# Two value tables with the far embedding in them, a plain transpose of the output, and chunks 10 slots apart

## The chip, the cores and the metric

The program runs on one core of a Trainium2 chip. The metric is the device time of one execution, in microseconds. Five engines take part: TensorE (PE, with its weight loads shown apart as PEld), VectorE (DVE), ScalarE (ACT), GpSimd (POOL) and the DMA queue of SyncE (SP). Each engine runs its own list of instructions in order and waits on semaphores for the others.

## The reference

```python
# x: (8, 1024, 256), 16 heads of 16 columns, relative distances clipped to -64..64
def attn(x):                                   # x is layernorm(x)
    q, k, v = (x @ W.T + b, split into heads)
    logits = q @ k.T + einsum('bhqd,qkd->bhqk', q, embK[clip(k - q) + 64])
    w = softmax(logits)
    out = w @ v + einsum('bhqk,qkd->bhqd', w, embV[clip(k - q) + 64])
    return out @ Wo.T + bo
x = x + layernorm(attn(layernorm(x)))
x = x + layernorm(layernorm(x) @ (ternary(Wf) * alpha).T + bf)
```

For a key more than 64 tokens away, the row of embV that is added is always the first (far to the left) or the last (far to the right). These two rows are "the far embedding". Since every weight of a query is used once, the far part of the output is: the sum of the weights on the left side times embV[0], plus the sum on the right side times embV[128].

## The kernel before, in words

A batch has 1024 tokens, in 8 tiles of 128 and in 4 chunks of 256. The 16 heads are two groups of 8. A step `s` is one query tile of one group of one batch, so there are 8 x 2 x 8 = 128 steps; 4 steps are a quad, 2 a pair. Per head of a step, TensorE computes a row of scores for the maximum (`row_max`, L736), DVE adds the band and takes the maximum of the two halves (L1013, L1016), TensorE computes the logits again transposed (`weights`, L759 and L764), ACT takes the exponent (L1216), and TensorE multiplies the weights with the values (`weighted`, L797). Four heads lie side by side in 32 rows each of the PSUM bank `oacc`.

The values lie in a ring of `VRING` = 4 buffers `vs`, one for each group of a batch. A head has 16 columns of value and 2 columns of ones. A tile on the left of the query takes 17 of these columns (`VL`), one on the right takes all 18 (`VR`), so that row 16 of the result is the sum of all weights and row 17 the sum of those on the right. Because row 17 is written by tiles on the right alone, the product starts with such a tile (`turns`), and for query tile 0 a matmul with zeros (L782) comes first. `out_copy` (ACT, L1223) moves a pair to `oT`, `relative` and `relative_sum` add the near embedding, and `out_norm` (L834) turns `oT` with a matmul against the 128x128 table `outmap`: the identity, with rows 16 and 17 of each head block holding the far embedding. DVE then divides by the sum (L1064, L1072).

The next batch is prepared in chunks beside the attention of the present one. The stages of a chunk are `load_x` (SP), `statistics` (DVE, then the root on POOL, L1244 to L1254), `normalise` (POOL, L869), `turn_x` (L683), `project_q` and `project_k` (L693), `far` (L701), `project_v` (L710), whose result DVE moves with the bias added to `vs` (L994, two instructions), the split into three bf16 parts on POOL (L885 to L893), and the writes to DRAM by SP (`write_q`, `write_far`, `write_k`; L502, L566), from which `load_q` and `load_k` fetch what the attention needs. `fraw`, a scratch of `far`, is a part of the chunk's input buffer `xc`. After the second group of a batch, each of its tiles goes through a tail: `tail_wo`, `tail_x1`, `tail_norm`, `tail_normed`, `tail_x1T`, `tail_ff`, `tail_out`, with three more roots on POOL.

The order of work on each engine is planned before the kernel is built. `timetable` (L105) gives each stage a slot; a batch of attention is 128 slots; `with_banks` moves a stage to a later slot when none of the three PSUM banks `misc` is free (with held times such as 1.8 slots for `project_v`), `LAG` adds an engine's delay, and each engine's list is the stages sorted by slot. A slot is no time: it only sets the order. The chunks of the next batch start at slots 40, 53, 72 and 85 of the present one. The tails of a batch take slots 101 to 173 from its start, so the last ones fall in slots 0 to 45 of the next batch. `relative` of a quad stands at its slot 29.6 on, `relative_sum` at 33, `out_norm` at 34.8 and 36.

Of the kernel before, what the change touches and what calls it, by code (L numbers as in the profile page):

```python
# [18 lines left out]
G = 2  # L19
# [16 lines left out]
VL, VR = D + 1, D + 2  # L36
# [5 lines left out]
QRING, BRING, VRING = 5, 7, 4  # L42
# [62 lines left out]
def timetable():  # L105
# [204 lines left out]
def build(nc, a, out):  # L310
    with ExitStack() as ctx:
# [17 lines left out]
        bv = sb("bv", [P, H])  # L329
        outmap = sb("outmap", [P, P])  # L330
# [3 lines left out]
        headmask, kfar = sb("headmask", [P, 32]), sb("kfar", [P, 2])  # L334
# [8 lines left out]
        vs = [sb(f"vs{i}", [P, T, HG, VR]) for i in range(VRING)]  # L343
# [25 lines left out]
        fraw = xc[:, 0, 0:P]  # L369
# [29 lines left out]
        band_cleared, ones_set, outmap_ready = sem("band_cleared"), sem("ones_set"), sem("outmap_ready")  # L399
# [16 lines left out]
        N_CONST, N_TABLE, N_ZERO = 8, 12, 8  # L416
# [90 lines left out]
        def sync_program(e):  # L507
# [5 lines left out]
            for t_, name in ((bq, "bq"), (bk, "bk"), (headmask, "headmask"), (kfar, "kfar")):  # L513
                e.dma_start(t_[:], a[name]).then_inc(const_in, 16)
            e.dma_start(bv[:], a["bv"].partition_broadcast(P)).then_inc(const_in, 16)
# [4 lines left out]
            for t_, name in ((later[:], "later"), (outmap[:], "outbase"), (zbuf[0][:, 0:P], "outleft")):  # L520
                e.dma_start(t_, a[name]).then_inc(table_in, 16)
            for t_, name in ((relmask[:], "relmask"), (relsel[:], "relsel"), (partmask, "partmask"), (embk6, "embk6")):
                e.dma_start(t_, a[name]).then_inc(table_in, 16)
# [16 lines left out]
            for stage, k in order:  # L540
# [120 lines left out]
        def tensor_program(e):  # L661
            pe, order = Engine(e), orders["PE"]
            for stage, k in order:
# [103 lines left out]
                elif stage == "weighted":  # L767
# [8 lines left out]
                    zero = zeros[:].bitcast(BF16)  # L776
# [586 lines left out]
```

## Time and profile before

| | us |
|---|---|
| three runs, median | 2812.86 |
| lowest, highest | 2808.33, 2814.58 |
| the profiled execution | 2808.32 |
| its span | 2806.5 |

The span is the time from the first to the last instruction in the trace, 1.8 us less than the execution's own time. The profile's page has one line for each view; the numbers behind an instruction are its busy time (in which instructions of one group that overlap count once), the mean length of one, and the idle time of the engine ahead of it. Matmuls overlap, so the length of one (some 275 ns) says little on how often one can start. What one costs is read from the distance of starts in the timeline.

### The profile page before, as it was taken

Reading aid. Unit: us, or ns where it says so; the run is one execution under the profiler, and the core shown is the slowest. Engines: PE = TensorE matmul, PEld = TensorE weight load, DVE = VectorE, ACT = ScalarE, POOL = GpSimd, SP = SyncE. Lnnn points to the kernel's source line nnn. Section 1 sums busy time; section 2 is a strip of 40 time slices with the busy share of each in tenths; the row PEclk is TensorE's granted clock in tenths of the full one; section 3 lists DMA queues with packets and bytes.
Section 4 is the critical chain, followed back from the end, with each engine's and each line's share of the span. In section 5 each row is a group of like instructions: output and inputs, shape, how many; then the busy total and the mean of one; then the engine's idle time right before and its main releaser. Section 6 shows DMA issues by size and latency. Waiting matters only on the chain.

```text
span 2806.5 us, 102954 instructions
## 1 busy us (share of the span) xinstructions
PE 2611.6 (93%) x43410; PEld 1965.8 (70%) x43410; DVE 2034.6 (72%) x5187; ACT 1557.5 (55%) x2993; POOL 959.2 (34%) x2275
## 2 busy tenths in 40 slices
PE   5899999999999999999999999999999999999995
PEld 3577777677776777767776777767777677777773
DVE  3776678776786778866787667876678766787774
ACT  2455556455555555555555565545665455565651
POOL 3113333433334323343234332334323433341026
PEclk8799999999999999999999999999999999999997
DMA  7556654456455564455645556446554456545410
GB/s 221 174 137 178 170 150 131 129 154 187 124 151 138 160 166 134 135 157 156 175 116 145 156 157 169 117 131 177 163 144 131 121 171 181 145 132 144 134 44 28
DMA packets 605048, 409.11 MB, mean 146 GB/s; under 512 B 149162, under 2 KB 604330, under 8 KB 604330
## 3 DMA queue, kind: packets, MB, share of 16 engines
q1 hardware_dynamic: 604586, 402.54, 50.7%
q8 instruction: 341, 5.59, 0.9%
q14 instruction: 121, 0.99, 0.1%
HBM read 206.84 MB, written 194.90 MB: 143 GB/s over the span
## 4 chain that ended last, share of the span: by engine, by line
PE 69%; DVE 16%; issue 5%; ACT 4%; POOL 3%; SPq 2%; DMA 1%; DVEq 0%; ACTq 0%; POOLq 0%
PE oacc L797 15%; PE logitsT L759 15%; PE scores L736 14%; PE logitsT L764 7%; DVE maxes L1016 6%; DVE junk L1013 5%; PE misc L860 4%; PE misc L693 4%; PE misc L822 2%; PE misc L834 2%; PE misc L710 2%; PE misc L810 2%; ACT wxr L1216 2%; POOL rs L1249 1%; PE misc L720 1%
## 5 line engine op out<-in xcount | busy, mean ns | idle before, releaser
L1013 DVE CUSTOM_DVE_ANT_1 junk<-scores,bands 128x512 bf16<-128x512 f32 x988 | 679.6, 688 | 585.3 <-PE scores L736 566.7
L759 PE MATMUL logitsT<-qs,ks 98*128 98x128 bf16 (+3 forms) x9088 | 994.9, 215 | 32.4 <-ACT wxr L1216 23.3
L1216 ACT ACTIVATE wxr<-logitsT 128x512 f32<-128x512 f32 x1024 | 599.8, 601 | 559.4 <-PE logitsT L759 463.0
L759 PEld LDWEIGHTS logitsT<-qs,ks 98*128 98x128 bf16 (+1 forms) x9088 | 679.5, 99 | 253.2 <-issue 92.8
L1216 ACT ACTIVATE wy<-logitsT 128x512 f32<-128x512 f32 x1024 | 587.4, 597 | 431.7 <-PE logitsT L759 421.3
L736 PE MATMUL scores<-ks,qs 101*128 101x256 bf16 (+10 forms) x4096 | 719.2, 291 | 77.3 <-DVE maxes L1016 38.4
L1016 DVE TENSOR_REDUCE maxes<-scores 128x1 f32<-128x512 f32 x1024 | 701.6, 685 | 1.9 <-PE scores L736 1.9
L736 PEld LDWEIGHTS scores<-ks,qs 96*128 96x128 bf16 (+3 forms) x4096 | 299.1, 99 | 263.7 <-DVE maxes L1016 119.5
L764 PE MATMUL logitsT<-ident,bands 128*128 128x128 f32 x2048 | 467.6, 280 | 0.0
L1244 POOL TENSOR_SCALAR rs<-rs 128x1 int32<-128x1 int32 (+1 forms) x224 | 48.6, 217 | 981.3 <-DVE rs L924 978.7
L764 PEld LDWEIGHTS logitsT<-ident,bands 128*128 128x128 f32 x2048 | 292.3, 143 | 33.2 <-issue 0.4
L1249 POOL TENSOR_SCALAR rs<-rs 128x1 f32<-128x1 f32 x768 | 292.4, 384 | 67.0
L797 PE MATMUL oacc<-wy,vs 128*17 128x128 f32 (+3 forms) x9216 | 276.5, 263 | 0.9 <-ACT wy L1216 0.9
L797 PE MATMUL oacc<-wxr,vs 128*18 128x128 f32 (+3 forms) x9216 | 276.6, 263 | 0.2
L797 PEld LDWEIGHTS oacc<-wy,vs 128*17 128x17 f32 (+1 forms) x9216 | 207.0, 98 | 45.2 <-issue 19.8
L1254 POOL TENSOR_SCALAR rs<-rs 128x1 f32<-128x1 f32 x768 | 212.0, 279 | 68.4
L797 PEld LDWEIGHTS oacc<-wxr,vs 128*18 128x18 f32 (+1 forms) x9216 | 206.9, 98 | 38.5 <-issue 23.5
L1038 DVE COPY_PREDICATED wxr<-later,wxr 128x512 f32<-128x512 int32 x224 | 174.8, 781 | 6.5 <-PE oacc L797 6.1
L1193 ACT ACTIVATE praw<-misc 128x512 f32<-128x512 f32 x256 | 152.7, 597 | 30.0 <-DMA bs<-praw 15.5
L1194 ACT ACTIVATE praw<-misc 128x512 f32<-128x512 f32 x256 | 155.4, 607 | 0.0
L1304 POOL TENSOR_TENSOR x<-ybuf,x 128x256 f32<-128x256 f32 x60 | 47.0, 783 | 192.5 <-DVE ybuf L1095 188.1
L810 PE MATMUL misc<-wxr,reltab 128*32 128x64 f32 x4096 | 102.9, 241 | 6.0 <-DVE wxr L1041 2.1
(136 smaller groups left out, 2561.5 us busy)
## 6 DMA issues: line engine op xcount, KB each, us to landing
bs<-praw SPq DMA_DIRECT2D x256, 512.0 KB, 4.3
bands<-bs SPq DMA_DIRECT2D x224, 512.0 KB, 4.3
ks<-kd SPq DMA_DIRECT2D x64, 384.0 KB, 5.0
qs<-qd SPq DMA_DIRECT2D x112, 192.0 KB
bands<-bs SPq DMA_DIRECT2D x128, 128.0 KB, 3.7
qd<-qparts SPq DMA_DIRECT2D x64, 192.0 KB, 3.2
kd<-kparts SPq DMA_DIRECT2D x64, 192.0 KB, 2.6
qd<-qparts SPq DMA_DIRECT2D x64, 128.0 KB, 2.6
```

The source lines that it names most:

```text
L736: mm = e.matmul(scores[r0:r1, c:c + length], qs[i][0:depth, h, r0:r1], kk[0:depth, h, key:key + length], start=True, stop=True, skip_group ...
L759: mm = e.matmul(lt[:, c * P + q0:c * P + q1], kk[0:depth, h, kt * P:(kt + 1) * P], qs[i][0:depth, h, q0:q1], start=q0 == 0, stop=not near, ...
L764: mm = e.matmul(lt[:, c * P:(c + 1) * P], band[v % BRING][:, h % HB, c * P:(c + 1) * P], ident[:], start=False, stop=True, is_transpose=Tr ...
L797: mm = e.matmul(oacc[32 * j:32 * j + (VR if right else VL), o0 + q0:o0 + q1], vs[m_ % VRING][:, kt, h, 0:VR if right else VL], src, start= ...
L810: mm = e.matmul(m[32 * j:32 * j + 32, o0:o0 + QUAD * HG * 2], reltab[:, 126 - q:128 - q, :].rearrange("p n d -> p (n d)"), wx[:, :, :, P + ...
L1013: e.tensor_tensor_reduce(junk[:], scores[:, 0:512].rearrange("p (a c) -> p a c", a=2), banded, 1.0, LOWEST, ALU.add, ALU.max, mx[:, h, 0:1 ...
L1016: e.tensor_reduce(mx[:, h, 1:2], scores[:, 512:S], AX.X, ALU.max).then_inc(row_maxed, 1)
L1038: e.copy_predicated(right, mask.bitcast(I32), left).then_inc(merged, 1)
L1194: e.activation(dst[:, :, P:WIN], src[:, :, P - 1:P].broadcast_to([P, HB, P]), ACT.Copy).then_inc(praw_ready, 1)
L1216: e.activation(dst, src, ACT.Exp).then_inc(exp_ready, 1)
L1249: op = e.tensor_scalar(rs[k][:, 3, x:x + 1], rs[k][:, 2, x:x + 1], rs[k][:, 0, x:x + 1], rs[k][:, 2, x:x + 1], ALU.mult, ALU.mult)
L1254: op = e.tensor_scalar(rs[k][:, 2, x:x + 1], rs[k][:, 3, x:x + 1], 1.5, rs[k][:, 2, x:x + 1], ALU.add, ALU.mult)
```

## The change

The values get two versions for each group, one for tiles on the left with bias + embV[0], one for tiles on the right with bias + embV[128]. Each has 16 columns of value and 1 of ones (`VW` = 17). All products have 17 rows, the matmul with zeros and the order `turns` go, and `out_norm` is a transpose by the identity. DVE writes four instructions for a chunk in place of two. The ring has 3 buffers. The chunks start at slots 61, 71, 81 and 91, with `project_k` and `write_k` 2 slots sooner within a chunk. `fraw` has a buffer of its own, and `load_x` no longer waits for `far`. At the start one more constant is loaded (`farV`, two rows broadcast to 128 partitions) and two tables less.

```diff
-VL, VR = D + 1, D + 2
+VW = D + 1
-QRING, BRING, VRING = 5, 7, 4
+QRING, BRING, VRING = 5, 7, 3
...
-            first = (b - 1) * G * T * HG + (40, 53, 72, 85)[c] if b else 10 * c - 100
+            first = (b - 1) * G * T * HG + (61, 71, 81, 91)[c] if b else 10 * c - 100
...
-                                 (2.3, "project_v"), (3.9, "far"), (6.5, "write_q"), (10.3, "project_k"),
-                                 (7, "write_far"), (13, "write_k")):
+                                 (2.3, "project_v"), (3.9, "far"), (6.5, "write_q"), (8.3, "project_k"),
+                                 (7, "write_far"), (11, "write_k")):
...
-        bv = sb("bv", [P, H])
-        outmap = sb("outmap", [P, P])
+        bvs = sb("bvs", [P, 2, H])
...
-        vs = [sb(f"vs{i}", [P, T, HG, VR]) for i in range(VRING)]
+        vs = [sb(f"vs{i}", [P, 2, T, HG, VW]) for i in range(VRING)]
...
-        fraw = xc[:, 0, 0:P]
+        fraw = sb("fraw", [P, P])[:]
+        headmask = fraw[:, 0:32]
...
-        N_CONST, N_TABLE, N_ZERO = 8, 12, 8
+        N_CONST, N_TABLE, N_ZERO = 9, 10, 8
...
-            e.dma_start(bv[:], a["bv"].partition_broadcast(P)).then_inc(const_in, 16)
+            e.dma_start(zbuf[0][:], a["bv"].partition_broadcast(P)).then_inc(const_in, 16)
+            e.dma_start(bvs[:].rearrange("p a h -> p (a h)"), a["farV"].partition_broadcast(P)).then_inc(const_in, 16)
...
-            for t_, name in ((later[:], "later"), (outmap[:], "outbase"), (zbuf[0][:, 0:P], "outleft")):
...
                     sp.wait_ge(x_turned, n("x_turned", "turn_x", b, c) - 1)
-                    sp.wait_ge(far_ready, b * NCHUNK + c)
                     e.dma_start(xc[:], xrow[b, c]).then_inc(x_in, 16)
...
-                    if kind == "X" and blk == 0 and t == 0:
-                        pe.wait_ge(band_cleared, 1)
-                        cols = oacc[:].rearrange("p (i q) -> p i q", i=4)[:, s % 2 * 2:s % 2 * 2 + 2, 0:HALF]
-                        e.matmul(cols, zero[:, 0:P], zero[:, 0:P], start=first, stop=True, skip_group_check=True)
-                        first = False
...
-                    turns = [1, 2, 3, 0] if kind == "X" and t else range(4)
-                    for x, c in enumerate(turns):
-                        kt = tiles[c]
+                    for c, kt in enumerate(tiles):
...
-                                mm = e.matmul(oacc[32 * j:32 * j + (VR if right else VL), o0 + q0:o0 + q1],
-                                              vs[m_ % VRING][:, kt, h, 0:VR if right else VL], src, start=first and x == 0,
-                                              stop=True, skip_group_check=True)
+                                mm = e.matmul(oacc[32 * j:32 * j + VW, o0 + q0:o0 + q1], vs[m_ % VRING][:, int(right), kt, h, :],
+                                              src, start=first and c == 0, stop=True, skip_group_check=True)
...
-                            mm = e.matmul(m[:, o0:o0 + P], oT[:, blk, pair % 2 * 2 + i, :], outmap[:], start=True, stop=True)
+                            mm = e.matmul(m[:, o0:o0 + P], oT[:, blk, pair % 2 * 2 + i, :], ident[:], start=True, stop=True,
+                                          is_transpose=True)
...
+                    e.tensor_tensor(bvs[:], bvs[:], zbuf[0][:].rearrange("p (a h) -> p a h", a=1).broadcast_to([P, 2, H]),
+                                    ALU.add).then_inc(bvs_ready, 1)
...
-                    then_step(e.tensor_tensor(outmap[:], outmap[:], zbuf[0][:, 0:P], ALU.subtract))
-                    dve.wait_ge(dve_step, step[0])
-                    e.tensor_tensor(outmap[:], outmap[:], ident[:], ALU.add).then_inc(outmap_ready, 1)
...
-                        op = e.tensor_tensor(
-                            vs[m_ % VRING][:, c * CHUNK:(c + 1) * CHUNK, :, 0:D],
-                            m[:, 0:CHUNK * H].rearrange("p (i g h d) -> p g i h d", i=CHUNK, g=G, h=HG)[:, g],
-                            bv[:, g * P:(g + 1) * P].rearrange("p (a h d) -> p a h d", a=1, h=HG)
-                            .broadcast_to([P, CHUNK, HG, D]), ALU.add)
+                        for side in range(2):
+                            op = e.tensor_tensor(
+                                vs[m_ % VRING][:, side, c * CHUNK:(c + 1) * CHUNK, :, 0:D],
+                                m[:, 0:CHUNK * H].rearrange("p (i g h d) -> p g i h d", i=CHUNK, g=G, h=HG)[:, g],
+                                bvs[:, side, g * P:(g + 1) * P].rearrange("p (a h d) -> p a h d", a=1, h=HG)
+                                .broadcast_to([P, CHUNK, HG, D]), ALU.add)
...
+        "farV": np.concatenate([np.tile(embV[0], NH), np.tile(embV[-1], NH)]),
```

## Rows read from the trace of the kernel before

**Rows 1.** The profile's page: busy time by engine, chain by engine.
```profile
PE 2611.6 (93%) x43410; PEld 1965.8 (70%) x43410; DVE 2034.6 (72%) x5187; ACT 1557.5 (55%) x2993; POOL 959.2 (34%) x2275
...
PE 69%; DVE 16%; issue 5%; ACT 4%; POOL 3%; SPq 2%; DMA 1%; DVEq 0%; ACTq 0%; POOLq 0%
```

**Rows 2.** Window of one batch: stretch, busy us of each engine, granted clock, DMA.
```profile
776.00:1114.00 338.00, 321.88 (x5428) 243.34 (x5426) 250.73 (x641) 192.75 (x372) 123.84 (x289) 1.00 0.53 149
```

**Rows 3.** Waits of the whole span, those of PE on DVE.
```profile
PE scores L736 <- DVE maxes L1016: 38.4, 185, 0.4
PE scores L736 <- DVE maxes L1013: 27.6, 58, 1.6
```

**Rows 4.** Timeline of PE: product with outmap, a transpose of four, what follows each.
```profile
1021.66 1.05 PE L834 MATMUL misc<-outmap,oT 128*128 128x128 f32 x8
1022.55 0.39 PE L759 MATMUL logitsT<-qs,ks 98*128 98x128 bf16 x4
...
902.46 0.61 PE L683 MATMUL misc<-ident,xc 128*128 128x128 f32 x4
902.90 0.39 PE L720 MATMUL misc<-bandtab,qs 96*128 96x128 bf16 x4
```

**Rows 5.** Groups by line: the output's product and the transposes.
```profile
L764 PE MATMUL logitsT<-ident,bands 128*128 128x128 f32 x2048 | 467.6, 280 | 0.0
...
L834 PE MATMUL misc<-outmap,oT 128*128 128x128 f32 x512 | 70.3, 280 | 7.9 <-DVE zbuf L1124 5.8 <-DVE oT L1056 2.1
```

**Rows 6.** Timeline of PE around the matmul with zeros.
```profile
236.75 0.22 PE L782 MATMUL oacc<-bands 128*128 128x128 bf16 x1
236.90 0.81 PE L797 MATMUL oacc<-wxr,vs 128*17 128x64 f32 x44
```

**Rows 7.** Groups by line: the value products of 18 and of 17 columns.
```profile
L797 PE MATMUL oacc<-wxr,vs 128*18 128x128 f32 x4608 | 170.8, 276 | 0.0
...
L797 PE MATMUL oacc<-wy,vs 128*17 128x128 f32 x4608 | 164.0, 276 | 0.0
```

**Rows 8.** DVE moves a chunk's values: timeline of one chunk.
```profile
878.74 0.75 DVE L994 TENSOR_TENSOR vs<-misc,bv 128x256 f32<-128x256 f32 x2
```

**Rows 9.** Windows of 26 us: two phases, each with chunks, then without.
```profile
848.00:874.00 26.00, 22.64 (x296) 16.28 (x291) 18.54 (x52) 13.06 (x25) 12.68 (x31) 1.00 0.33 91
2538.00:2564.00 26.00, 25.07 (x382) 18.60 (x381) 21.47 (x58) 15.81 (x29) 6.65 (x18) 1.00 0.40 112
...
900.00:926.00 26.00, 25.38 (x581) 20.03 (x581) 18.56 (x44) 16.26 (x33) 8.09 (x11) 1.00 0.57 172
2590.00:2616.00 26.00, 25.30 (x679) 19.57 (x678) 21.45 (x53) 13.23 (x25) 0.00 (x0) 1.00 0.46 135
```

**Rows 10.** Timeline near 860 us: two roots on POOL, then DVE and PE.
```profile
853.16 0.19 POOL L1244 TENSOR_SCALAR rs<-rs 128x2 int32<-128x2 int32 x1 [0.43 <-DVE rs L924]
856.15 0.15 DVE L924 TENSOR_SCALAR rs<-mv 128x1 f32<-128x1 f32 x1
858.03 0.19 POOL L1244 TENSOR_SCALAR rs<-rs 128x1 int32<-128x1 int32 x1
860.77 0.79 DVE L1117 TENSOR_SCALAR zbuf<-x,mv,rs 128x256 f32<-128x256 f32 x1 [1.03 <-POOL rs L1254]
862.23 0.39 PE L736 MATMUL scores<-ks,qs 96*128 96x256 bf16 x2 [1.59 <-DVE maxes L1013]
```

**Rows 11.** Timeline of one chunk after its transpose at 902.46 us: ACT, SP, POOL.
```profile
909.14 0.83 ACT L1171 ACTIVATE qf<-misc,bq 128x256 f32<-128x256 f32 x2
926.81 1.36 SPq L566 DMA_DIRECT2D qd<-kparts  x4
930.44 0.85 ACT L1171 ACTIVATE qf<-misc,bk 128x256 f32<-128x256 f32 x2 [5.53 <-PE misc L693]
933.99 1.16 POOL L893 TENSOR_TENSOR kparts<-qf,kparts 128x512 bf16<-128x512 f32 x1
```

**Rows 12.** Chain of waits at the start of the span.
```profile
12.61 4.74 DMA alpha<-in_alpha
```

More of the change, by code:

```diff
@@ L333, in build @@
         relmask, relsel = sb("relmask", [P, 2]), sb("relsel", [P, 4, 32])
-        headmask, kfar = sb("headmask", [P, 32]), sb("kfar", [P, 2])
+        kfar = sb("kfar", [P, 2])
         farw = sb("farw", [P, 32])
@@ L398, in build @@
         far_first, far_second, far_ready = sem("far_first"), sem("far_second"), sem("far_ready")
-        band_cleared, ones_set, outmap_ready = sem("band_cleared"), sem("ones_set"), sem("outmap_ready")
+        band_cleared, ones_set, bvs_ready = sem("band_cleared"), sem("ones_set"), sem("bvs_ready")
         farw_ready, k_ones_in, v_ones_set, junk_set = sem("farw_ready"), sem("k_ones_in"), sem("v_ones_set"), sem("junk_set")
@@ L512, in sync_program @@
                 e.dma_start(t_[:], a[name].rearrange("(i p) o -> p i o", p=P)).then_inc(const_in, 16)
-            for t_, name in ((bq, "bq"), (bk, "bk"), (headmask, "headmask"), (kfar, "kfar")):
-                e.dma_start(t_[:], a[name]).then_inc(const_in, 16)
-            e.dma_start(bv[:], a["bv"].partition_broadcast(P)).then_inc(const_in, 16)
+            for t_, name in ((bq[:], "bq"), (bk[:], "bk"), (headmask, "headmask"), (kfar[:], "kfar")):
+                e.dma_start(t_, a[name]).then_inc(const_in, 16)
+            e.dma_start(zbuf[0][:], a["bv"].partition_broadcast(P)).then_inc(const_in, 16)
+            e.dma_start(bvs[:].rearrange("p a h -> p (a h)"), a["farV"].partition_broadcast(P)).then_inc(const_in, 16)
             for c in range(1, NCHUNK):
@@ L519, in sync_program @@
                 e.dma_start(t_[:], a[name].rearrange("(i p) o -> p i o", p=P)).then_inc(table_in, 16)
-            for t_, name in ((later[:], "later"), (outmap[:], "outbase"), (zbuf[0][:, 0:P], "outleft")):
-                e.dma_start(t_, a[name]).then_inc(table_in, 16)
-            for t_, name in ((relmask[:], "relmask"), (relsel[:], "relsel"), (partmask, "partmask"), (embk6, "embk6")):
+            for t_, name in ((later[:], "later"), (relmask[:], "relmask"), (relsel[:], "relsel"), (partmask, "partmask"), (embk6, "embk6")):
                 e.dma_start(t_, a[name]).then_inc(table_in, 16)
@@ L775, in tensor_program @@
                     pe.wait_ge(v_ones_set, 1)
-                    zero = zeros[:].bitcast(BF16)
                     if first and s >= 2:
                         pe.wait_ge(o_copied, s // 2)
-                    if kind == "X" and blk == 0 and t == 0:
-                        pe.wait_ge(band_cleared, 1)
-                        cols = oacc[:].rearrange("p (i q) -> p i q", i=4)[:, s % 2 * 2:s % 2 * 2 + 2, 0:HALF]
-                        e.matmul(cols, zero[:, 0:P], zero[:, 0:P], start=first, stop=True, skip_group_check=True)
-                        first = False
                     o0 = (s % 2 * 2 + blk) * P
-                    turns = [1, 2, 3, 0] if kind == "X" and t else range(4)
-                    for x, c in enumerate(turns):
-                        kt = tiles[c]
+                    for c, kt in enumerate(tiles):
                         for q0, q1, right in value_sides(t, kt):
@@ L828, in tensor_program @@
                     pe.wait_ge(o_added, 2 * (pair // 2) + 2)
-                    pe.wait_ge(outmap_ready, 1)
                     pe.wait_ge(*free)
@@ L933, in vector_program @@
                     dve.wait_ge(dve_step, step[0])
-                    e.tensor_scalar(farw[:], headmask[:], small[:, 4:5], None, ALU.mult).then_inc(farw_ready, 1)
+                    e.tensor_scalar(farw[:], headmask, small[:, 4:5], None, ALU.mult).then_inc(farw_ready, 1)
+                    e.tensor_tensor(bvs[:], bvs[:], zbuf[0][:].rearrange("p (a h) -> p a h", a=1).broadcast_to([P, 2, H]),
+                                    ALU.add).then_inc(bvs_ready, 1)
                 elif stage == "tables":
@@ L989, in vector_program @@
                     dve.wait_ge(v_summed, n("v_summed", "project_v", b, c))
+                    dve.wait_ge(bvs_ready, 1)
                     for g in range(G):
@@ L1264, in pool_program @@
             for t_ in vs:
-                op = e.memset(t_[:, :, :, D:VR], 1.0)
+                op = e.memset(t_[:, :, :, :, D:VW].rearrange("p a t h c -> p (a t h) c"), 1.0)
             op.then_inc(v_ones_set, 1)
@@ L1333 @@
     f32 = np.float32
-    outbase, outleft = np.zeros((P, P), f32), np.zeros((P, P), f32)
-    for r in range(0, P, 32):
-        outbase[r + D, r:r + D], outbase[r + D + 1, r:r + D], outleft[r + D + 1, r:r + D] = embV[0], embV[-1], embV[0]
     ins = {
```

3 lines of the change are left out of this document (removed).

## The prediction

> **What bounds the kernel now.** I read the page first: PE is busy 93% of the span, DVE 72%, and the chain that ended last lies to 69% on PE and to 16% on DVE [rows 1]. The windows say that this is even: in the 338 us of one batch PE is busy 321.9 us at a granted clock of 1.00, DVE 250.7 us, POOL 123.8 us [rows 2]. So a slot is 338 / 128 = 2.64 us, PE idles 16 us in a batch, and what is taken off PE comes off the span unless PE then waits. The waits show for what: for DVE's maxima, 38.4 + 27.6 = 66 us over the whole span, in 243 short pieces [rows 3]. DVE is thus the second bound, near enough that what is added to it can't be free everywhere. The last view is windows of the same phase in different batches, which show where PE idles more than elsewhere [rows 9].
>
> **Part 1, the transpose in out_norm.** The product with `outmap` takes 8 matmul instructions for 4 tiles; from its first start to the next instruction's is 1022.55 - 1021.66 = 0.89 us. Four float32 transposes by the identity, the same shapes, take 902.90 - 902.46 = 0.44 us [rows 4]. The saving is 0.45 us for each pair, and there are 64 pairs: 28.8 us of PE. Some will be lost where PE came to the pair late by a wait on DVE (7.9 us of idle in all ahead of L834 [rows 5]); half of the pairs stand among tails, where DVE is fuller. I take 90%, -26 us; bounds -29 and -18.
>
> On this the Trainium skill speaks twice. Trace first: L764 makes 2048 float32 transposes of 128x128 of 280 ns each, but they keep PE busy for only 467.6 us, 228 ns each with their overlaps [rows 5], in windows whose granted clock is 1.00 [rows 2]. The page "TensorE: Matmul & The Clock Gate", Part 4: PE-mode transpose, says that a transpose takes about 275 ns in a kernel and doesn't count as PE activity for the clock. By the length alone, paid in full, the sum would not fall but rise (a rival below). The table of terms of the same page says that the transpose mode is 4 times faster for float32; by that the pair would fall from 0.89 to 0.22 us, and the sum would be 14 us better than mine. The rows show a factor of two.
>
> **Part 2, the values.** A product of 18 columns costs what one of 17 does, 276 ns both [rows 7]; the columns are not what PE is paid for, so the uniform 17 give nothing. The matmuls with zeros are 16, each 236.90 - 236.75 = 0.15 us to the next start [rows 6]: -2.4 us, I take -2. The order of the four tiles changes no count.
>
> DVE pays. Two instructions for a chunk's values take 0.75 us with their overlap [rows 8]; four take 2 x 0.75 less one overlap, about 1.43 us. That is +0.68 us for each of 32 chunks, 21.8 us of DVE. Behind them in DVE's list stand the next maxima, for which PE waits. Outside the tails DVE is busy 18.56 of 26 us [rows 9], so it has room to catch up within some microseconds; the cover is that idle time. PE's waits for DVE are 66 of 2806 us, and mostly beside tails, from which the new slots stay away. I take a sixth, +3.5 us; bounds 0 and +21.8. The bank that holds the product is freed 0.7 us later, inside the 1.8 slots (4.8 us) that the planner holds it.
>
> The ring of three buffers brings a wait on the products of the group three before. For the second group of the next batch that is the first group of the present one, whose last product has slot 53.6 + 3.5 + 4.1 = 61.2. `project_v` of the first chunk has slot 63.3 on PE, behind it in the same list, and DVE needs that result anyway. The wait is over when it is reached: 0. From slot 40 it would not have been, which is why the chunks move.
>
> **Part 3, the chunks at slots 61 to 91.** This is the part with a gain that the words of the change don't name. At 848 to 874 us (slots 33 to 43 of a batch) a chunk's statistics meet the last tails, and PE is busy 22.64 of 26 us. In the last batch, which has these tails but no next chunk, the same phase (2538 to 2564) shows 25.07 [rows 9]. The mechanism can be read in one place: POOL starts the root of the chunk at 853.16 and that of the tail only at 858.03, though its input was there at 856.15 + 0.15; DVE waits for it 1.03 us at 860.77, and PE 1.59 us for DVE at 862.23 [rows 10]. The new first chunk starts 21 slots later, when no tail is near. That is 2.43 us in each of the six batches that have both: -14.6 us. What chunks cost elsewhere: with a chunk PE is busy 25.38 of 26 us, at the same phase without any 25.30 [rows 9], so PE does them with no idle time of their own. Against the gain stands the other end: the last chunk's work now runs to slot 102, and the first tail begins at 101. The split of its keys on POOL (slot 101.3) is still ahead of the tail's first root (103.8). Two chunks now also fall on `relative` (slots 61.6 and 93.6); by slots this shifts `project_v` by 0.4 at most, and PE has the work of both to do in any order. I take -11 us; bounds -17 and +10.
>
> `load_x` without its wait and `fraw` apart take nothing off the path: with 10 slots between chunks the old wait would also have been over. 0.
>
> **Part 4, the start.** SP issues 10 table loads for 12, and one constant more. What PE waits for is the last one, `alpha`, issued at 12.61 and landed 4.74 us later [rows 12]; it is issued one load earlier, some 0.5 us. The add of `farV` (about 0.7 us of DVE) falls into DVE's wait for the root of the second chunk. -0.5 us; bounds -1 and +1.5.
>
> **The sum.** -26 - 2 + 3.5 - 11 - 0.5 = -36 us. The profiled execution took 2808.3 us (span 2806.5 and 1.8 around it), which gives 2772. It is the lowest of the range of runs; their median is 2812.9, from which the same sum gives 2777. I say 2775, and reckon the rivals from the same 2811.
>
> **The rivals.** (a) The move is worth nothing, since the new place has collisions of its own: -26 - 2 + 3.5 - 0.5 = -25, 2786. For it: POOL's list holds the key split just ahead of the tail's root. Against: in the chunkless batch the PE idles no less than with chunks [rows 9]. (b) DVE becomes the bound and all of its 21.8 us show: -36 + 18 = -18, 2793. For it the 66 us of waits; against, DVE's idle quarter in [rows 2]. (c) Transposes are paid at their length [rows 5]: 256 x 0.28 = 72 us for 64 x 0.89 = 57 now, so +15 for -26, and the sum is +5, 2816. That is the change not doing what it says. Against it the starts 0.44 / 4 = 0.11 us apart in [rows 4]. (d) **the other side:** chunks 10 slots (26.4 us) apart have no slack. ACT may not take the next chunk's queries out of PSUM before POOL has split the keys of this one. Counted from the transpose, ACT did that 6.7 us in, so for the next chunk it is due 26.4 + 6.7 = 33.1 us in. The keys came to POOL 28.8 us in, now 2 slots sooner, 23.5; the split took 3.8 us (to 935.15) and ended 32.7 us in, now at best 27.4. But it overwrites the buffer from which SP sends the far part, and SP had done issuing that at 25.7 us in [rows 11]; with 0 to 4.7 us to land (the latter is the small load of [rows 12]), the split starts at 25.7 to 30.4, say 28, and ends 3.8 us later, at 31.9. The slack is 1.2 us, within 5.7 and -1.1. If SP is later by more than that, ACT stands, exponents stop, and PE, which may run two blocks of logits ahead, stops too. There are 21 such passages (3 in each of 7 batches). From 1.8 us lost in each (36 / 21) the change is no gain; at 3 us it is -36 + 63 = +27, 2838. For it: SP is in order, and the example's SP was late by a wait for the maxima. Against: the attention's own SP work is no more than before, and the example is one with SP late.
>
> **How the numbers follow.** The forecast with its own range (2760 to 2786) has 0.58, (a) 0.16, (b) 0.08, (c) 0.04, (d) 0.07, and 0.07 that both savings come in full or more (-29 - 2.4 - 17 with the start, down to 2755). The range is 2756 to 2803: it takes in (a) and (b), and leaves out (c), (d) and the ends. A change within 0.2% (5.6 us) can't be told from none by such runs. Faster by more has 0.88, within it 0.06, which is (c) and a mild (d), slower 0.06.
>
> **What would show it.** `out_norm` with 256 matmul instructions for 512, and 0.44 us from its start to the next instruction. `vs` written by 128 DVE instructions, DVE busy some 20 us more. No L782. PE busy some 31 us less in all, and the window at slots 33 to 43 at about 25 of 26 us. Waits of PE for `maxes` that grow by less than 4 us. I am wrong in part 3 if a new hole in PE stands at slots 95 to 105 or ACT waits for POOL's split; in part 2 if PE's waits for DVE grow by 10 us or more; in part 1 if transposes start 0.2 us apart.

## The result, and the profile after

The changed kernel takes 2816.66 us (median of 20 runs, 2811.64 to 2822.67), the kernel before in the same sitting 2809.61 us (20 runs, 2805.70 to 2815.82). The ratio is 1.0024, with an interval from 1.0017 to 1.0031: slower by 0.24%, or 7 us. I had forecast 2775 us and a range of 2756 to 2803; both are wrong, and so is the sign. Of the twelve executions of one experiment below, the doubled add at the old slots, one took 4688.02 us, in a slower state, and counts in no ratio.

The page of the changed kernel, its span, busy time by engine and chain by engine, against [rows 1]:

```profile
span 2813.6 us, 102464 instructions
...
PE 2588.7 (92%) x43138; PEld 1933.5 (69%) x43138; DVE 2057.9 (73%) x5250; ACT 1558.8 (55%) x2993; POOL 953.6 (34%) x2274
...
PE 60%; DVE 26%; issue 6%; ACT 4%; POOL 2%; SPq 1%; DMA 1%; DVEq 0%; POOLq 0%; ACTq 0%
```

PE lost 22.9 us of work (2611.6 to 2588.7) and the span still grew by 7.1: PE's idle time went from 194.9 to 224.9 us, +30. DVE gained 23.3 us of work, and its share of the chain rose from 16% to 26%. Something that had cover before has none now. The waits of PE on DVE, which answer to [rows 3]:

```profile
PE scores L734 <- DVE maxes L1004: 46.5, 224, 0.4
PE scores L734 <- DVE maxes L1001: 30.1, 69, 1.5
```

They grew from 66.0 to 76.6 us, so of the 30 us of new idle time 10.6 stand here; the rest is spread over smaller waits. Two of these are for PSUM banks that DVE has yet to empty, in seven places each: ahead of `project_v` (L708), a wait that the kernel before does not have, and ahead of `relative` (L799), which with one version of the values (an experiment below) is the last row:

```profile
PE misc L708 <- DVE relout L1035: 6.5, 7, 0.9
PE misc L799 <- DVE vs L982: 6.4, 7, 0.9
...
PE misc L799 <- DVE vs L982: 1.7, 7, 0.2
```

Groups by line of the changed kernel (busy us, mean ns of one | idle before, releaser), the first of which answers to [rows 5]; of before, the merge of the mask, COPY_PREDICATED on DVE, is the last row below:

```profile
L822 PE MATMUL misc<-ident,oT 128*128 128x128 f32 x256 | 39.8, 278 | 13.7 <-DVE zbuf L1112 5.8 <-ACT praw L1182 4.6 <-DVE oT L1044 3.3
L799 PE MATMUL misc<-wxr,reltab 128*32 128x64 f32 x4096 | 101.7, 241 | 10.4 <-DVE vs L982 6.4 <-DVE wxr L1029 1.9 <-DVE wxr L1026 1.7
L982 DVE TENSOR_TENSOR vs<-misc,bvs 128x256 f32<-128x256 f32 x128 | 45.0, 414 | 0.0
L1026 DVE COPY_PREDICATED wxr<-later,wxr 128x512 f32<-128x512 int32 x224 | 191.1, 853 | 12.6 <-PE oacc L787 12.6
```

```profile
L1038 DVE COPY_PREDICATED wxr<-later,wxr 128x512 f32<-128x512 int32 x224 | 174.8, 781 | 6.5 <-PE oacc L797 6.1
```

`out_norm` has its 256 matmuls, and PE comes late to them: 13.7 us of idle time for 7.9. The 128 adds are there. What I had not looked for is the merge: the same 224 instructions take 16.3 us more than before.

To see where in a batch the time goes, I cut each of batches 1 to 6 at the first `out_norm` instruction of each query quad (about slots 34.8, 66.8, 98.8 and 130.8) and took the mean length and, in brackets, the mean of all idle time of PE in each piece (batches 2 to 6 for the first piece). The pieces are named by their slots; nearly all of the new chunks' work lies in the last three. Each row is of one execution, so differences of some 0.1 us say nothing. In us, with the experiments of the next section beside them:

```
kernel                 to 34.8       35 to 67      67 to 99      99 to 131     batch
before                 82.45 (4.50)  90.66 (4.75)  82.30 (3.03)  83.06 (3.44)  338.47
transpose alone        82.11 (5.06)  91.19 (5.41)  82.08 (3.47)  82.13 (3.47)  337.51
new slots alone        82.77 (4.52)  81.04 (3.73)  88.19 (3.20)  85.56 (4.04)  337.56
slots + second add     82.19 (4.52)  81.70 (4.17)  91.55 (5.34)  85.74 (4.14)  341.18
after, one version     82.10 (5.06)  81.36 (4.61)  87.10 (3.21)  84.59 (4.03)  335.16
after                  82.41 (5.06)  81.68 (4.79)  90.57 (5.37)  84.73 (4.08)  339.39
```

### The profile page after: what moved, and what is told of

The parts are those of the page before. It is cut to its first block, busy times and chain, and to the rows that moved or that the text cites. A ratio compares the mean times of both kernels' runs of the same rounds, so it can differ in the third digit from the quotient of the medians.

```text
span 2813.6 us, 102464 instructions
## 1 busy us (share of the span) xinstructions
PE 2588.7 (92%) x43138; PEld 1933.5 (69%) x43138; DVE 2057.9 (73%) x5250; ACT 1558.8 (55%) x2993; POOL 953.6 (34%) x2274
## 4 chain that ended last, share of the span: by engine, by line
PE 60%; DVE 26%; issue 6%; ACT 4%; POOL 2%; SPq 1%; DMA 1%; DVEq 0%; POOLq 0%; ACTq 0%
PE oacc L787 13%; PE logitsT L757 13%; PE scores L734 12%; DVE maxes L1004 9%; DVE junk L1001 8%; PE logitsT L762 6%; PE misc L849 4%; PE misc L691 4%; PE misc L811 2%; DVE stats L908 2%; PE misc L708 2%; ACT wxr L1204 2%; PE misc L799 1%; DVE wxr L1026 1%; DVE vs L982 1%
## 5 line engine op out<-in xcount | busy, mean ns | idle before, releaser
L734 PE MATMUL scores<-ks,qs 101*128 101x256 bf16 (+10 forms) x4096 | 728.4, 292 | 91.2 <-DVE maxes L1004 46.5
L1237 POOL TENSOR_SCALAR rs<-rs 128x1 f32<-128x1 f32 x768 | 279.1, 366 | 67.0
L787 PE MATMUL oacc<-wxr,vs 128*17 128x128 f32 (+1 forms) x9216 | 277.5, 264 | 0.3 <-issue 0.3
L787 PE MATMUL oacc<-wy,vs 128*17 128x128 f32 (+1 forms) x9216 | 274.0, 262 | 1.4 <-ACT wy L1204 1.2
L1242 POOL TENSOR_SCALAR rs<-rs 128x1 f32<-128x1 f32 x768 | 219.4, 289 | 68.2
L787 PEld LDWEIGHTS oacc<-wy,vs 128*17 128x17 f32 x9216 | 205.7, 97 | 41.6 <-issue 19.2
L787 PEld LDWEIGHTS oacc<-wxr,vs 128*17 128x17 f32 x9216 | 207.6, 98 | 38.0 <-issue 21.7
L1026 DVE COPY_PREDICATED wxr<-later,wxr 128x512 f32<-128x512 int32 x224 | 191.1, 853 | 12.6 <-PE oacc L787 12.6
L799 PE MATMUL misc<-wxr,reltab 128*32 128x64 f32 x4096 | 101.7, 241 | 10.4 <-DVE vs L982 6.4
```

Source lines behind the costliest of these rows:

```text
L734: mm = e.matmul(scores[r0:r1, c:c + length], qs[i][0:depth, h, r0:r1], kk[0:depth, h, key:key + length], start=True, stop=True, skip_group ...
L787: mm = e.matmul(oacc[32 * j:32 * j + VW, o0 + q0:o0 + q1], vs[m_ % VRING][:, int(right), kt, h, :], src, start=first and c == 0, stop=True ...
L1026: e.copy_predicated(right, mask.bitcast(I32), left).then_inc(merged, 1)
L1237: op = e.tensor_scalar(rs[k][:, 3, x:x + 1], rs[k][:, 2, x:x + 1], rs[k][:, 0, x:x + 1], rs[k][:, 2, x:x + 1], ALU.mult, ALU.mult)
L1242: op = e.tensor_scalar(rs[k][:, 2, x:x + 1], rs[k][:, 3, x:x + 1], 1.5, rs[k][:, 2, x:x + 1], ALU.add, ALU.mult)
```

## The experiments

Each ratio is to the kernel before in the same sitting. The first of them take the change apart.

**The transpose alone.** The kernel before with `out_norm` by identity transposes; the far embedding is left out.

```diff
-  e.matmul(m[:, o0:o0 + P], oT[...], outmap[:], start=True, stop=True)
+  e.matmul(m[:, o0:o0 + P], oT[...], ident[:], start=True, stop=True, is_transpose=True)
```

> The kernel before, with out_norm as a transpose by the identity and nothing else (the far embedding is left out). Theory A (each pair saves its 0.45 us of PE and PE is the bound): -26 us, ratio 0.991. Theory B (where DVE is the second bound the saving comes back as waits; the quads without chunks of the last batch moved by -0.09, -0.95 and -0.35 us for 0.9 each): -8 to -16 us, ratio 0.995 to 0.997.

Measured: 2799.79 us, ratio 0.9963 [0.9950, 0.9976], so -10.4 us. The price of the instruction was as forecast. Timeline of PE in this kernel:

```profile
937.85 0.60 PE L834 MATMUL misc<-ident,oT 128*128 128x128 f32 x4
938.29 0.39 PE L759 MATMUL logitsT<-qs,ks 101*128 101x128 bf16 x4
...
857.53 0.39 PE L720 MATMUL misc<-bandtab,qs 96*128 96x128 bf16 x4
859.50 0.39 PE L736 MATMUL scores<-ks,qs 96*128 96x256 bf16 x2 [1.58 <-DVE maxes L1014]
...
862.35 1.61 PE L797 MATMUL oacc<-wy,vs 128*17 128x128 f32 x32
```

From the transposes' start to the next instruction's are 0.44 us, half of the product's 0.89 in [rows 4]. The last three rows, and the windows below (busy time of each engine, then the granted clock), show part of what was given back: PE stood for 1.58 us at the place of [rows 10], and right behind it the clock fell.

```profile
858.00:860.00 2.00, 0.39 (x2) 0.11 (x2) 1.96 (x5) 1.30 (x3) 2.00 (x4) 1.00 0.18 64
860.00:862.00 2.00, 1.90 (x12) 1.42 (x12) 1.86 (x5) 0.40 (x1) 1.67 (x1) 0.53 0.69 189
862.00:864.00 2.00, 2.00 (x36) 1.39 (x35) 0.00 (x0) 0.80 (x2) 0.00 (x0) 0.62 1.21 275
864.00:866.00 2.00, 2.00 (x21) 1.70 (x20) 1.47 (x4) 0.56 (x2) 0.00 (x0) 1.00 0.32 109
```

At 0.53 and 0.62 most of the stretch ran at 1.2 GHz for 2.4; 32 value products took 1.61 us for the 1.07 of the other blocks, and by my estimate from the two windows (2 x 0.47 + 2 x 0.38) some 1.7 us are lost in all. The kernel before, at the same phase of this batch, stood for 1.59 us [rows 10] and kept its clock; such a fall stands in its trace at this phase in three batches, in this kernel's in five. So the length of the stop does not tell by itself whether the clock falls; what decides it is open. PE's busy time fell by 22.0 us (2611.6 to 2589.6), not by 28.8; two or three more falls make up 3 to 5 of the difference. The other loss is idle time: the waits for maxima rose from 66.0 to 76.7 us here too. In the table each piece has two pairs, 0.9 us to win. Only the last one keeps it (-0.93); the first keeps 0.34, the third 0.22, and the second, which begins with the place of [rows 10], is longer by 0.53.

**One version of the values.** The changed kernel without its second add; the products of right blocks read the left version, so they get the left side's far embedding and the right side's is left out.

```diff
-  vs[m_ % VRING][:, int(right), kt, h, :]
+  vs[m_ % VRING][:, 0, kt, h, :]
-  for side in range(2):
+  for side in range(1):
```

> The changed kernel with only the left version of the values written and used (the far right embedding is left out), so 64 DVE instructions less, all else as changed. The changed kernel is at 1.0024 of before. Theory A (DVE's second add shows for a sixth): -3.5 us, ratio 1.001. Theory C (the second add is what spoils it, all 21.8 us show): ratio 0.995.

Measured: 2789.59 us, 0.9925 [0.9911, 0.9940]. Against the changed kernel's 1.0024 this is -27.8 us for 64 adds. DVE's busy time is 2024.1 us, 33.8 less, though the adds are only 45.0 - 23.9 = 21.1 us of it; the merges (177.7 us in this kernel) are 13.4, which is all of the rest. Of the 224 merges 25 take over 0.9 us in this kernel and 42 in the changed one, and in both traces each of these overlaps a TENSOR_TENSOR of POOL. PE's busy time is 2578.1 us, 10.6 less for the same matmuls; the changed kernel's clock falls three times near slot 88, this one's at no such place, which is some 5 us of it.

**The second add alone, at the old slots and at the new.** The first kernel is the one before, with each add made once more into a spare tile; the second is the one before with the new slots, `fraw` in a tile of its own and `load_x` without its wait; the third is both.

```diff
+  dve.wait_ge(v_ready, b * NCHUNK + c)                        # first and third; DVE's own count
+  e.tensor_tensor(spare[:, g], m[...], bv[...], ALU.add)      # first and third, ahead of the add into vs
...
-  first = (b - 1) * G * T * HG + (40, 53, 72, 85)[c] if b else 10 * c - 100
+  first = (b - 1) * G * T * HG + (61, 71, 81, 91)[c] if b else 10 * c - 100
-  (10.3, "project_k"), (13, "write_k")
+  (8.3, "project_k"), (11, "write_k")
-  fraw = xc[:, 0, 0:P]
+  fraw = sb("fraw", [P, P])[:]
-  sp.wait_ge(far_ready, b * NCHUNK + c)
```

> The kernel before, with every add of project_v on DVE done twice (the other time into a spare buffer), at the old slots. Theory A: +3.5 us, ratio 1.001. Theory C (all of the 21.8 us show): ratio 1.007. If it is near 1.000 here while the same instructions cost more in the changed kernel, the slots are what makes them dear.

> The kernel before with the chunks at slots 61 to 91 and the two shifts within a chunk; fraw has its own buffer and load_x does not wait for far, which these slots need; all else as before. Theory D (the move itself is a gain, as the forecast had it, and what spoils the change is the second add on DVE in its new place): the one-version kernel at 0.9925 less the transpose's 0.0037 leaves ratio 0.996. Theory B (the move collides with relative and costs): ratio 1.002 to 1.005.

> As the run with the move alone, with every add of project_v done twice (the other into a spare buffer). At the old slots this cost nothing (0.9997). Theory D: the same adds cost 20 to 27 us here, ratio 1.003 to 1.006, COPY_PREDICATED longer than 0.83 us on average. Theory E (it was not the adds but reading two versions of the values that cost the changed kernel 27 us): ratio as with the move alone, 0.996.

Measured: the add at the old slots 2808.78 us (median of the eleven that count), 0.9997 [0.9986, 1.0007]; the new slots alone 2804.62 us, 0.9983 [0.9973, 0.9992]; both 2833.78 us, 1.0084 [1.0066, 1.0101]. The same 64 instructions cost nothing at the old slots and 28 us at the new. The three pages' busy times and their merges, in this order:

```profile
PE 2607.3 (93%) x43410; PEld 1963.2 (70%) x43410; DVE 2047.6 (73%) x5251; ACT 1557.4 (56%) x2993; POOL 958.9 (34%) x2275
...
L1045 DVE COPY_PREDICATED wxr<-later,wxr 128x512 f32<-128x512 int32 x224 | 171.7, 767 | 6.4 <-PE oacc L798 5.9
```

```profile
PE 2607.0 (93%) x43410; PEld 1967.6 (70%) x43410; DVE 2026.6 (72%) x5187; ACT 1557.7 (56%) x2993; POOL 959.3 (34%) x2275
...
L1037 DVE COPY_PREDICATED wxr<-later,wxr 128x512 f32<-128x512 int32 x224 | 179.3, 800 | 12.6 <-PE oacc L796 12.6
```

```profile
PE 2609.8 (92%) x43410; PEld 1965.3 (70%) x43410; DVE 2057.2 (73%) x5251; ACT 1558.8 (55%) x2993; POOL 958.3 (34%) x2275
...
L1044 DVE COPY_PREDICATED wxr<-later,wxr 128x512 f32<-128x512 int32 x224 | 189.5, 846 | 12.6 <-PE oacc L797 12.6
```

At the old slots DVE's busy time grows by 13.0 us and the merges shrink by 3.1; at the new, by 30.6, with 10.2 in the merges. And there the 30.6 us of DVE come out as 28 us of time, more than the 20 to 27 that I had expected. This kernel's products read one version of the values, so the price is not that of reading two.

The new slots with `fraw` left in `xc` and `load_x` left waiting for `far` give a kernel that stops for good in a ring of waits. With chunks 10 slots apart POOL's list has the root of the next chunk (5 slots from the chunk's start) ahead of this chunk's `far` (5.9); the root waits for `load_x`, and `load_x` for `far`. So these two edits are a part of the move, and no run has the move without them.

**Why the place matters.** Each add stands in DVE's list behind a maximum, and what counts is the next wait behind it. In the kernel before, timeline of DVE behind three of the four adds of one batch (the first of them, at 878.74, is in [rows 8]):

```profile
880.49 0.69 DVE L1013 CUSTOM_DVE_ANT_1 junk<-scores,bands 128x512 bf16<-128x512 f32 x1 [1.00 <-PE scores L736]
...
963.56 0.74 DVE L994 TENSOR_TENSOR vs<-misc,bv 128x256 f32<-128x256 f32 x2
964.81 0.69 DVE L1013 CUSTOM_DVE_ANT_1 junk<-scores,bands 128x512 bf16<-128x512 f32 x1 [0.51 <-PE scores L736]
...
996.42 0.75 DVE L994 TENSOR_TENSOR vs<-misc,bv 128x256 f32<-128x256 f32 x2
997.20 0.69 DVE L1013 CUSTOM_DVE_ANT_1 junk<-scores,bands 128x512 bf16<-128x512 f32 x1
...
998.42 1.55 DVE L1038 COPY_PREDICATED wxr<-later,wxr 128x512 f32<-128x512 int32 x1
```

DVE waits for PE's scores for 1.00 and 0.51 us behind two of them: 0.66 us more fit in, wholly or nearly. (Behind the second of the four, at 913.39, it waits 0.16.) Behind the fourth there is no wait close by, but a merge of 1.55 us; with the doubled add it starts later and takes 1.03. Summed over the waits for scores that end within 6 us behind each of the four adds, a usual batch of the kernel before has 2.22, 0.55, 1.69 and 0.66 us, 5.1 in all, for the 2.6 that four doubled adds ask. With the new slots alone the same sums are 1.35, 0.71, 0.28 and 0, 2.3 in all. The adds start there at 924.78, 956.21, 982.54 and 1011.01 us; the three waits:

```profile
929.49 0.69 DVE L1012 CUSTOM_DVE_ANT_1 junk<-scores,bands 128x512 bf16<-128x512 f32 x1 [1.35 <-PE scores L735]
959.49 0.69 DVE L1012 CUSTOM_DVE_ANT_1 junk<-scores,bands 128x512 bf16<-128x512 f32 x1 [0.71 <-PE scores L735]
984.90 0.69 DVE L1012 CUSTOM_DVE_ANT_1 junk<-scores,bands 128x512 bf16<-128x512 f32 x1 [0.28 <-PE scores L735]
```

In the changed kernel the second and third of these are gone and the first still stands, at 1.29 us: by the time DVE came to it PE had been held up too. This fits the prices, but the two kernels differ in more than these waits, and no run moves one add alone against its wait. Now the changed kernel, DVE and then POOL around one of the new places:

```profile
956.29 1.41 DVE L982 TENSOR_TENSOR vs<-misc,bvs 128x256 f32<-128x256 f32 x4
957.62 1.50 DVE L1026 COPY_PREDICATED wxr<-later,wxr 128x512 f32<-128x512 int32 x1
959.02 0.67 DVE L1001 CUSTOM_DVE_ANT_1 junk<-scores,bands 128x512 bf16<-128x512 f32 x1
...
957.36 1.16 POOL L878 TENSOR_TENSOR qf<-qf,qparts 128x512 f32<-128x512 f32 x1 [4.96 <-PE misc L699]
```

The same place with one version of the values, DVE and POOL:

```profile
949.26 0.74 DVE L982 TENSOR_TENSOR vs<-misc,bvs 128x256 f32<-128x256 f32 x2
949.92 0.73 DVE L1026 COPY_PREDICATED wxr<-later,wxr 128x512 f32<-128x512 int32 x1
950.54 0.68 DVE L1001 CUSTOM_DVE_ANT_1 junk<-scores,bands 128x512 bf16<-128x512 f32 x1
...
950.33 1.31 POOL L878 TENSOR_TENSOR qf<-qf,qparts 128x512 f32<-128x512 f32 x1 [4.95 <-PE misc L699]
```

With one version the merge starts before POOL's subtraction and takes 0.73 us. With two it starts 0.26 us behind POOL's and takes 1.50, to 0.60 us past POOL's end at 958.52. From the add's start to the next maximum's are 1.28 us in the one and 2.73 in the other: 0.67 of add and 0.78 of merge, with no wait for PE between them to take any of it. Behind the batch's next add it is so again: the merge takes 1.64 us at 987.45 in the changed kernel, and 0.81 at 979.18 with one version.

The Trainium skill, page "SBUF — State Buffer", section "SBUF: two separate sides", says that VectorE, in an operation with two SBUF inputs, and GpSimd, in one that reads SBUF, take a shared port pair as an exclusive lock for the whole instruction. The trace agrees: 1.50 us is a merge of 0.73 that stood for about 0.8.

A smaller part of the price lies at the banks: PE's wait ahead of `relative` for DVE's values is 6.4 us for 1.7 with one version, and that ahead of `relative_sum` for `relout` 5.4 for 2.5, together 7.6 of the 28 us.

**Is it the lock, or the adds' own length?** The changed kernel with POOL's split of queries and keys made on a quarter of the columns from the second batch on (the other columns keep old data). It leaves DVE's list as it is and takes away most of what holds it.

```diff
+  w_ = CT // 4 if b else CT
-  e.tensor_tensor(qf[:], qf[:], qp[:, 0], ALU.subtract)
+  e.tensor_tensor(qf[:, :, 0:w_], qf[:, :, 0:w_], qp[:, 0, :, 0:w_], ALU.subtract)   # and so the other three
```

> The changed kernel with POOL's instructions of the split on a quarter of the columns from the second batch on (the rest of the parts keeps old data). Theory D with the lock (a merge that starts while POOL's two-input instruction runs waits for its end; three such merges a batch take 1.5 to 1.6 us for 0.73): all merges near 0.73 to 0.85 us, mean below 0.78, and -12 to -17 us, ratio 0.996 to 0.998. If the long merges have another cause they stay near 0.853 on average, and the time at 1.0024.

Measured: 2801.77 us, 0.9976 [0.9967, 0.9985], 13.5 us less than the changed kernel. The merges:

```profile
L1027 DVE COPY_PREDICATED wxr<-later,wxr 128x512 f32<-128x512 int32 x224 | 170.9, 763 | 12.6 <-PE oacc L787 12.6
```

They fall by 20.2 us, DVE's busy time by 19.9 (to 2038.0). So at most about half of the 27.8 us hangs on POOL's holding DVE, and the rest, 14.3 us from here to the kernel with one version, on the adds themselves and on what follows from them. It is an upper bound, since this edit also frees merges that POOL holds with one version (170.9 us here, 177.7 there); one version with the short split, which would part the two, was not run. The split's end may also come sooner for SP and ACT by this edit; the run doesn't part that either.

**The add behind the merge.** The lag of `project_v` on DVE is 1.5 slots for 1.0, which puts the adds one place later.

```diff
-    "DVE": {"project_v": 1.0, ...
+    "DVE": {"project_v": 1.5, ...
```

> The changed kernel with DVE's lag of project_v at 1.5 slots for 1.0, which puts the adds of the second chunk behind a merge (COPY_PREDICATED) instead of ahead of it; same instructions. Theory D (the adds push a merge into POOL's split, where it takes 1.50 for 0.73 us): one merge a batch short again and the maxima sooner, -5 to -12 us against the changed kernel's 1.0024, so 0.998 to 1.001. Theory F (DVE's time is paid in whatever order): 1.002 to 1.003.

Measured: 2816.73 us, 1.0024 [1.0014, 1.0034]: nothing, for the 5 to 12 us expected. The merges did get cheaper, 180.7 us for 191.1, and DVE's busy time fell by 10.0 us. PE's rose instead, from 2588.7 to 2596.5 us. Its timeline near slot 88 and the windows there:

```profile
993.13 0.39 PE L734 MATMUL scores<-ks,qs 96*128 96x256 bf16 x2 [1.60 <-DVE maxes L1001]
```

```profile
994.00:996.00 2.00, 2.00 (x20) 0.98 (x22) 1.86 (x6) 1.09 (x2) 1.69 (x7) 0.55 1.13 325
996.00:998.00 2.00, 2.00 (x40) 1.38 (x32) 0.59 (x1) 0.00 (x0) 1.75 (x6) 0.59 1.15 342
```

PE stands for 1.60 us, where it stood for 1.13 in the changed kernel at 991.06, which kept a clock of 1.00 in that batch; then it runs at 0.55 and 0.59. This fall is in six of the seven places of the phase, for three in the changed kernel; at 1.7 us each the three more are some 5 of the 7.8 us. So most of what DVE gained stands in this trace as PE's clock. The trace is of the slowest of this kernel's twelve executions (2820.32 us), and the others may have fewer falls.

**The first chunk's values later.** `project_v` of the first chunk 5.6 slots behind the chunk's start for 2.3, of the last 10.6, both behind `relative` and `relative_sum`. This tests the rival that the shared PSUM banks are what costs.

```diff
-  (2.3, "project_v")
+  ((5.6, 2.3, 2.3, 10.6)[c], "project_v")
```

> The changed kernel with project_v of the first chunk 3.3 slots later and of the last chunk 8.3 slots later, both behind relative and relative_sum; same instructions. PE waited 1.08 + 0.39 us a batch at project_v and relative_sum for DVE's relout, and 1.07 us at relative for DVE's vs. Theory B (the shared banks): these 2.5 us times 7 batches go, -15 to -18 us, ratio 0.996. Theory D alone (only the second and third chunk matter): -3 to +3 us, ratio 1.0015 to 1.0035.

Measured: 2811.04 us, 1.0004 [0.9994, 1.0014], 5.6 us less than the changed kernel. The waits ahead of `project_v` for `relout` and ahead of `relative` for the values are gone from its trace (those for `praw` ahead of `out_norm` grew from 4.6 to 9.2 us), and yet the gain is a third of what I had expected of them. In pieces: slots 35 to 67 -2.38, 67 to 99 -0.33, 99 to 131 +1.88 us a batch. The last chunk's add only lands among the next piece's maxima, and whether the first move pays by itself is for the second of the next two kernels to tell.

**The second version on POOL.** Neither of the two experiments above found room in DVE's list for both. POOL is busy 34% of the span. Here DVE writes the left version alone, and POOL adds the difference of the far embeddings to it for the right one, behind the next chunk's `normalise` in its list; all is computed. The second kernel has `project_v` of the first chunk at 5.6 slots as well.

```diff
+  "POOL": {..., "project_v": 5.7, ...
-  for side in range(2):
+  for side in range(1):
+  elif stage == "project_v":        # POOL
+      pool.wait_ge(v_ready, n("v_ready", "project_v", b, c))
+      for g in range(G):
+          op = e.tensor_tensor(v_[:, 1, chunk], v_[:, 0, chunk], bvs[:, 1, ...], ALU.add)
+      op.then_inc(v_right, 1)       # PE waits for it instead of v_ready
```

> The changed kernel with the second version of the values made by POOL: DVE writes the left one from PSUM (two instructions a chunk, as before), and POOL adds the difference of the two far rows to it in SBUF (two instructions a chunk, behind the next chunk's normalise in its list). All is computed. Theory D (what cost 27 us is 64 more instructions in DVE's list at places where it doesn't wait for PE; POOL has the time): near the one-version run, ratio 0.993 to 0.996. Theory G (the work costs wherever it is, because POOL then locks or delays DVE and its own splits): 0.999 to 1.003.

> As the run with the second version on POOL, and project_v of the first chunk 3.3 slots later, behind relative_sum. In the run that moved the first and the last chunk's values, the quad of the first lost 2.4 us a batch and that of the last gained nothing. Theory B (the shared banks at the first chunk cost 1.08 + 0.39 us a batch): 7 x 1.5 = -10 us against the run before it, ratio 0.990 to 0.992. Otherwise the same as it.

Measured: 2792.42 us, 0.9933 [0.9917, 0.9950], and 2793.32 us, 0.9943 [0.9927, 0.9958]. The first beats both kernels, the one before by 0.67% and the changed one by 0.9%; the second adds nothing to it: 1.86 us less a batch in slots 35 to 67 and 1.81 more in 67 to 99, so the later add of the first chunk pays nothing by itself. The page of the first, then its adds and merges by group:

```profile
PE 2578.5 (92%) x43138; PEld 1930.9 (69%) x43138; DVE 2027.3 (73%) x5187; ACT 1558.1 (56%) x2993; POOL 1001.6 (36%) x2338
```

```profile
L1273 POOL TENSOR_TENSOR vs<-vs,bvs 128x256 f32<-128x256 f32 x64 | 42.8, 691 | 12.0 <-DVE vs L984 12.0
L1028 DVE COPY_PREDICATED wxr<-later,wxr 128x512 f32<-128x512 int32 x224 | 179.2, 800 | 12.6 <-PE oacc L788 12.6
```

POOL pays 42.8 us for what cost DVE 21.1, and the kernel is 25 us faster: the ratio is within 0.0008 of the one that leaves the second version out.

What the experiments show of the cause is thus that the second add is dear at the new slots and not at the old, that it costs next to nothing once DVE neither makes it nor holds the bank for it, and that POOL's hold on the merges is at most half of it. How the rest divides between waits that are missing behind the adds, the banks and PE's clock is argued from the timelines.

## Why the prediction was wrong, step by step

**What bounds the kernel: right, but not used.** I wrote that PE's idle time is short of DVE's results and that DVE is the second bound. Then I priced DVE's new work by averages, its idle quarter and 66 us of waits, and took a sixth.

**Part 2, DVE's second add, is the step that failed.** The forecast was +3.5 us with bounds of 0 and +21.8. It measured +27.8 (one version against the changed kernel) and +28 (doubled add at the new slots); even my upper bound was too low. Its count was right: 128 instructions, +0.66 us each time. Two things were not. The cover was taken as DVE's idle time in the windows; but that time stands at certain waits, and close behind the adds at the new slots there are 2.3 us of them in a batch, for 5.1 at the old. And DVE's price for the merge was taken as fixed, when it depends on whether POOL is in a subtraction at that time: with two versions 17 merges more are held, about two and a half in each of seven batches (13.4 us in all, 0.8 each). I had also written that the bank with the product is freed late at no cost; PE's wait for it ahead of `relative` is 4.7 us longer than with one version. My test for this part, that PE's waits for maxima grow by 10 us or more, came out at +10.6, but by itself it proves nothing here, since the transpose alone gives +10.7. What shows it is the piece from slot 67 to 99: +3.47 us of length over the one with one version, +3.86 of DVE.

The rival that DVE becomes the bound and all of its 21.8 us show, with 0.08, was nearest to what happened, at 2793 for lack of the merges and because the other terms were too good.

At the old slots the same adds cost -1 us (interval -4 to +2): there even a sixth was too much. The move of the chunks, which I had as a gain of its own, is what took their cover. I argued for each part apart, and the ring of three buffers, for which I had a wait of 0, is why I took them to have to stand together; no run has three buffers, or two versions of the values in use, at the old slots.

**Part 1, the transpose: -26 forecast, -10.4 measured**, outside its bounds too (-29 to -18). The 0.44 us was right to the digit, and against the rival that transposes are paid at their length. I allowed 10% for PE's coming late. It was over half: a faster PE at a place where DVE's list sets the pace only waits sooner, and behind its stops at the phase of [rows 10] the clock fell in five batches for three.

**Part 3, the move: -11 forecast, -5 measured.** The gain at the collision is there. Windows of the changed kernel at the phase of [rows 9]:

```profile
848.00:874.00 26.00, 24.52 (x375) 17.25 (x370) 20.57 (x57) 14.95 (x28) 5.96 (x16) 1.00 0.44 115
```

PE is busy 24.52 us for 22.64, near the 25 I gave. What I had missed is what the chunk meets at its new end. I had named a new hole at slots 95 to 105 as a sign against me, and it came, at the second `out_norm` of slot 100, in six of the seven batches that have chunks beside them. Timeline of PE in the changed kernel:

```profile
1028.87 0.66 PE L822 MATMUL misc<-ident,oT 128*128 128x128 f32 x4 [0.77 <-ACT praw L1182]
```

Another stands at the chunk's start: 0.93 us ahead of `project_v` in each of seven batches, at the banks that it shares with `relative`. I had written that PE has the work of both to do in any order, and put the clash at nothing.

In the table the new slots alone take 1.02 us of idle time from the piece of slots 35 to 67, and put 0.17 and 0.60 back into the next two. That nets to about -0.2 of idle time and, with the clock's falls at [rows 10] gone, -0.9 us a batch. And `fraw` apart with `load_x` free, for which I had 0 because the old wait would have been over, is what lets the new slots run at all.

The rival for the other side, ACT's waiting for POOL's split because chunks stand 10 slots apart, did not happen: the new slots alone are no slower, and the wait that would show it is in none of the longest waits of the changed kernel. (36 / 21, from which I had the loss that makes the change no gain, is 1.7 and not 1.8.) The kernel went to the other side by another way, for which I had given 0.06.

**Part 4, the start: -0.5 forecast.** The first `out_norm` stands at 178.5 us for 177.7, and between 176.3 and 180.9 in the traces of the other kernels, so no gain can be seen, and one of half a microsecond would not show.

**The sum.** -10.4 (transpose) - 4.8 (move) + 27.8 (adds) leaves -5.9 us to reach the measured +6.7. That is what the matmuls with zeros (16, gone), the columns, the start, the interplay of the parts and the noise of three ratios share; I forecast -2.5 for them and did not part them. The profiled execution of the changed kernel says the same as the runs: span 2813.6 for 2806.5.

## What to carry to other kernels

Price an instruction that is added to a nearly full engine at its place, not by the engine's idle share: follow its list forward to the first wait that is long enough to take it, and take it as paid until then. Do this at the new place where the change also moves work; two parts that are each harmless can be dear together. And ask what else may lengthen on that engine when its phase against another one slips.

## What I had not expected of the hardware

A COPY_PREDICATED of 128x512 on DVE takes 0.73 us by itself and 1.50 to 1.64 us when it starts while POOL is in a TENSOR_TENSOR of SBUF operands (957.62 and 987.45 us of the changed kernel, 0.26 and 0.11 us behind a start of POOL's). All 42 merges of over 0.9 us in that trace overlap such an instruction.

Behind a single stop of PE of 1.58 or 1.60 us the granted clock fell, to 0.53 to 0.62 in the 4 us of windows shown; behind one of 1.13 us it did not, in the batch shown, and behind the one of 1.59 us in [rows 10] it did not either. By the windows a fall costs some 1.7 us more, as much as the stop itself.
